# A new step order for a pipelined linear-attention and mixture-of-experts block on one core

## The reference

```python
x = x + conv(ln_c(x))            # causal linear attention, 8 heads of 16
t = tokens(x)
t = t + ffn(ln_t(t))             # 8 experts, the best two of each token
# conv: q, k, v = W x + b;  Q, K = elu(.)+1
#   num_l = Q_l . sum_{j<=l} K_j V_j^T ;  den_l = Q_l . cumsum(K)_l
#   (K is summed over the axis that cumsum(axis=1) names: the heads)
# ffn: probs = softmax(xf @ gate_w + router); best two kept as weights
#   out = sum_e combine_e * (gamma_e * (xf @ expert_w[e] + expert_b[e]) + beta_e)
```

## Time and profile before

| what | before |
| --- | --- |
| median of 3 runs | 755.08 us (754.4 to 756.46) |
| the profiled execution's own time | 755.91 us |
| its span | 754.1 us |
| TensorE matmul busy | 717.1 us, 95% |
| VectorE busy | 685.9 us, 91% |
| ScalarE, GpSimd busy | 409.9 us and 397.8 us |
| mean granted TensorE clock | 0.982 of full speed |

### The profile page before, as it was taken

The page is one execution under the profiler, slowest core; times in us unless marked ns, Lnnn a source line. Parts: engine busy times, 40 slices in busy tenths (PEclk is TensorE's granted clock), DMA queues, the critical chain, the costliest instruction groups (busy, mean ns, idle before and its releaser), DMA issues.

```text
span 754.1 us, 23195 instructions
## 1 busy us (share of the span) xinstructions
PE 717.1 (95%) x8137; PEld 624.0 (83%) x8137; DVE 685.9 (91%) x2550; ACT 409.9 (54%) x1261; POOL 397.8 (53%) x639
## 2 busy tenths in 40 slices
PE   4767999999999999999999999999999999999986
PEld 2666888888888888888888888888888888888875
DVE  4567999999999999999999999999999999999984
ACT  1122666655555666666665555555555555555544
POOL 5145555555555555555555555555555555555520
PEclk9769999999999999999999999999999999999999
DMA  5101111111111111111111111111111111111101
GB/s 129 33 15 30 42 40 35 37 40 37 39 37 42 42 42 42 42 42 42 42 42 42 42 42 42 42 42 42 42 42 42 42 42 42 42 30 29 30 16 29
DMA packets 60214, 30.29 MB, mean 40 GB/s; under 512 B 2160, under 2 KB 60176, under 8 KB 60176
## 3 DMA queue, kind: packets, MB, share of 16 engines
q1 hardware_dynamic: 60176, 29.79, 14.4%
HBM read 20.34 MB, written 9.44 MB: 39 GB/s over the span
## 4 chain that ended last, share of the span: by engine, by line
PE 91%; DVE 4%; POOL 2%; ACT 1%; issue 1%; DMA 1%; SPq 0%; DVEq 0%; ACTq 0%; POOLq 0%
PE bank L877 11%; PE bank L915 10%; PE bank L894 9%; PE bank L916 9%; PE bank L917 9%; PE bank L933 8%; PE bank L901 4%; PE bank L909 4%; PE bank L884 4%; PE bank L853 3%; PE bank L854 3%; PE bank L855 3%; PE bank L860 3%; PE bank L847 2%; PE bank L866 2%; PE bank L935 2%
## 5 line engine op out<-in xcount | busy, mean ns | idle before, releaser
L574 DVE TENSOR_TENSOR probs<-bank,tri 128x512 f32<-128x512 f32 x288 | 184.9, 684 | 10.2 <-PE bank L877 4.7
L397 ACT ACTIVATE y_act<-bank,scale 128x128 f32<-128x128 f32 x576 | 159.4, 383 | 2.5
L915 PE MATMUL bank<-e_high,x_high 128*128 128x512 f32 x288 | 124.0, 431 | 1.1 <-DVE o L803 1.1
L916 PE MATMUL bank<-e_low,x_high 128*128 128x512 f32 x288 | 113.7, 395 | 0.0
L917 PE MATMUL bank<-e_high,x_low 128*128 128x512 f32 x288 | 113.5, 394 | 0.0
L311 POOL TENSOR_TENSOR qn<-feat,rden 128x512 f32<-128x512 f32 x36 | 38.2, 1061 | 116.4 <-DVE rden L672 116.4
L416 ACT ACTIVATE x_high<-x 128x512 fp32r<-128x512 f32 x36 | 22.8, 633 | 137.0 <-DVE x L664 137.0
L592 DVE SCALAR_TENSOR_TENSOR y_dve<-bank,scale,y_dve 128x128 f32<-128x128 f32 x288 | 92.4, 343 | 0.0
L580 DVE SCALAR_TENSOR_TENSOR qkv<-bank,rstd,b_qkv 128x384 f32<-128x384 f32 x144 | 86.8, 605 | 5.1 <-POOL rstd L301 2.6
L387 ACT ACTIVATE k_odd<-bank,parity 128x512 f32<-128x512 f32 x36 | 24.7, 687 | 114.4 <-PE bank L860 114.4
L933 PE MATMUL bank<-ident,y_act 128*128 128x128 f32 x576 | 80.8, 273 | 1.6 <-ACT y_act L397 1.6
(11 more groups left out here) (139 smaller groups left out, 1764.5 us busy)
## 6 DMA issues: line engine op xcount, KB each, us to landing
x<-in_x SPq DMA_DIRECT2D x36, 256.0 KB, 3.3
x_res<-in_x SPq DMA_DIRECT2D x36, 256.0 KB, 3.2
out<-o SPq DMA_DIRECT2D x36, 256.0 KB, 2.4
beta_raw<-in_L_ffn_beta_w SPq DMA_DIRECT2D x1, 512.0 KB
e_raw<-in_L_ffn_expert_w SPq DMA_DIRECT2D x1, 512.0 KB
w_raw<-in_L_conv_Wkv SPq DMA_DIRECT2D x2, 64.0 KB, 2.4
b_qkv<-in_L_conv_bkv SPq DMA_DIRECT2D x1, 128.0 KB, 4.4
w_raw<-in_L_conv_Wq SPq DMA_DIRECT2D x1, 64.0 KB, 2.6
```

The lines of the kernel that those rows point to most:

```text
L397: last = nc.scalar.activation(y_act[:, p, u, e], bank[EXPERTS_AT[u][0]][:, 128 * e:128 * e + 128], ACT.Copy, scale=scale[:, p, u, e:e + 1])
L574: return tt(probs[:, half, i].rearrange("p u e t -> p (u e) t"), bank[SCORES_AT[half][i]][:].rearrange("p (n t) -> p n t", t=T), tri[:].un ...
L915: mm(out, x1_high[:, p, u], e_high[:, w], start=True, stop=False)
L916: mm(out, x1_high[:, p, u], e_low[:, w], start=False, stop=False)
```

## The change

Every engine's step gets another order, and the banks are dealt out anew. TensorE's list in one step after: turn_k; values_1, values_0; proj_2, proj_0; experts_01; proj_1; turn_x1; experts_00, 11; proj_3; turn_q; turn_x of g[1]; experts_31, 21, 20; scores_1 of g[3]; experts_30; turn_coef; experts_10; key_values; from_state of g[3]; bias; scores_0 of g[3]; turn_y of units 2 and 3, then of units 0 and 1. So `scores_0` and `from_state` move from g[4] to g[3], and `turn_x` with its moments and `x_high` from g[0] to g[1]. The products are the same in number and size.

```diff
-AT = dict(x=4, kv=3, att=6, x1_a=6, x1_b=4, k=1, q=7, coef=0, out=1)
-PROJ_AT = (4, 0, 3, 2)
-SCORES_AT = ((3, 7, 2, 0), (0, 5, 6, 7))
-EXPERTS_AT = ((4, 2), (6, 5), (1, 1), (2, 3))
+AT = dict(x=5, kv=5, att=4, x1_a=0, x1_b=5, k=1, q=6, coef=3, out=0)
+PROJ_AT = (7, 3, 1, 4)
+SCORES_AT = ((3, 2, 7, 6), (1, 5, 7, 6))
+EXPERTS_AT = ((1, 2), (7, 7), (3, 4), (2, 0))
...
-            def turn_y(p, u):
-
-                out = bank[AT["out"]][:, T * u:T * u + T]
-                for e in range(4):
-                    mm(out, y_act[:, p, u, e], ident[:], start=False, stop=False, is_transpose=True,
-                       skip_group_check=True)
-                return mm(out, y_dve[:, p, u], ident[:], start=False, stop=True, is_transpose=True,
-                          skip_group_check=True)
+            def turn_y(p, half):
+
+                for e in range(5):
+                    for u in (2 * half, 2 * half + 1):
+                        last = mm(bank[AT["out"]][:, T * u:T * u + T], y_act[:, p, u, e] if e < 4 else y_dve[:, p, u],
+                                  ident[:], start=False, stop=(e == 4), is_transpose=True, skip_group_check=True)
+                return last
```

TensorE's waits of the new order that the text speaks of:

```diff
+                    need(pe, "y_dve_12", n - 1)
+                    need(pe, "y_act_0", n - 1)
+                    scores(p, 1).then_inc(S["scores_1"], 1)
...
+                    need(pe, "probs_12", n + 3)
+                    experts(p, 1, 0).then_inc(S["experts_10"], 1)
...
+                    need(pe, "probs_11", n + 1)
+                    key_values(p).then_inc(S["kv"], 1)
+                    need(pe, "y_dve_22", n - 1)
+                    from_state(p).then_inc(S["from_state"], 1)
```

More of the change, by code:

```diff
@@ L177, in program @@
         names = ("consts setup first_loaded rest_loaded first_pe first_dve rest_pe rest_dve x_eps x1_eps "
[4 rows of a table removed]
-                 "rank_b qkv_0 rank_b_max soft_scaled den_eps hot_b x1 hot_ab rden scale coef qkv_3 x_moments "
[5 rows of a table removed]
-                 "k_sum_3 x_rstd k_sum_4 k_sum_5 k_sum_6 k_sum_7 qk qn state coef_low x_low x1_rstd ").split()
+                 "k_turned values_1 values_0 proj_2 proj_0 experts_01 proj_1 x1_turned experts_00 experts_11 "
+                 "proj_3 q_turned x_turned experts_31 experts_21 experts_20 scores_1 experts_30 coef_turned "
+                 "experts_10 kv from_state bias scores_0 y_turned_b y_turned_a rank_b_max x1 qkv_2 hot_b soft "
+                 "den hot_ab soft_scaled den_eps qkv_0 rden coef scale x1_parts qkv_1 x1_moments qkv_3 "
[3 rows of a table added]
+                 "probs_01 out psum_r rank_b kv_new k_even k_odd x_high x1_high y_one_0 coef_high lg_raw_a "
+                 "lg_raw_b y_one_1 q_t y_act_0 y_one_3 exps_1 y_one_2 y_act_2 exps_0 y_act_3 coef_t y_act_1 "
+                 "v_pad_0 v_pad_1 k_sum_0 pexp x_low k_sum_2 k_sum_3 k_sum_4 k_sum_5 k_sum_6 k_sum_7 qk qn "
+                 "coef_low x1_low x1_rstd state x_rstd k_sum_1 ").split()
         S = {n: sem(n) for n in names}
@@ L777, in step @@
                 if g[3]:
-                    n = g[3].i
-                    need(dve, "scores_1", n + 1)
-                    causal(1, 1).then_inc(S["probs_11"], 1)
-                    causal(1, 0).then_inc(S["probs_10"], 1)
+                    causal(0, 1).then_inc(S["probs_01"], 1)
+                if g[5]:
+                    n, p = g[5].i, g[5].par
+                    need(dve, "y_turned_a", n + 1)
+                    need(dve, "y_turned_b", n + 1)
+                    if not isinstance(n, int) or n >= PAR:
+                        dve.wait_ge(stored[p], 16 * g[5].half)
+                    tt(flat(o, p), bank[AT["out"]][:], flat(x1, p), ALU.add).then_inc(S["out"], 1)
                 if g[4]:
@@ L879, in scores @@
                 return last
-            def from_state(p):
-                for u in range(U):
-                    last = mm(bank[AT["att"]][:, T * u:T * u + T], state[:, U * p + u], q_t[:, p, u],
-                              start=(u == 0), stop=False, skip_group_check=True)
-                return last
             def values(p, half):
@@ L895, in values, with from_state @@
                                       probs[:, half, i, v, e], start=False, stop=(e == 1), skip_group_check=True)
+                return last
+            def from_state(p):
+                for u in range(U):
+                    last = mm(bank[AT["att"]][:, T * u:T * u + T], state[:, U * p + u], q_t[:, p, u],
+                              start=(u == 0), stop=False, skip_group_check=True)
                 return last
@@ L1054, in step @@
                     turn_q().then_inc(S["q_turned"], 1)
+                if g[1]:
+                    n, p = g[1].i, g[1].par
+                    pe.wait_ge(x_loaded[p], 16 * (g[1].half + 1))
+                    need(pe, "lg_raw_b", n - 2)
+                    if k is not None:
+                        need(pe, "x_parts", n)
+                    turn_x(p).then_inc(S["x_turned"], 1)
+                if g[5]:
+                    n, p = g[5].i, g[5].par
+                    need(pe, "x1_parts", n + 2)
+                    need(pe, "lg_raw_a", n + 2)
+                    if k is not None:
+                        need(pe, "out", n)
+                    experts(p, 3, 1).then_inc(S["experts_31"], 1)
+                    need(pe, "qkv_3", n + 4)
+                    if k is not None:
+                        need(pe, "x1", n + 2)
+                        need(pe, "y_one_2", n)
+                        need(pe, "y_dve_22", n)
+                    experts(p, 2, 1).then_inc(S["experts_21"], 1)
+                    need(pe, "qkv_1", n + 4)
+                    if k is not None:
+                        need(pe, "probs_00", n + 2)
+                        need(pe, "coef_t", n)
+                    experts(p, 2, 0).then_inc(S["experts_20"], 1)
@@ new lines, in step @@
+                if g[3]:
+                    n, p = g[3].i, g[3].par
+                    need(pe, "probs_13", n + 1)
+                    need(pe, "y_act_3", n - 1)
+                    need(pe, "y_act_1", n - 1)
+                    if k is not None:
+                        need(pe, "qkv_1", n + 2)
+                        need(pe, "probs_01", n)
+                        need(pe, "probs_12", n + 1)
+                        need(pe, "qkv_0", n + 2)
+                    scores(p, 0).then_inc(S["scores_0"], 1)
```

597 lines of the change are left out of this document (267 added, 330 removed), and 12 rows, old and new, of the table names.

## The result

The changed kernel takes 761.02 us, median of five executions (758.07 to 762.63); the kernel before took 755.08 (754.09 to 757.15). The ratio is 1.0069, with a 95% interval of 1.0048 to 1.0090: the change makes the kernel 0.7% slower. I had forecast 751.0, with 746.5 to 760.0 as the range.

A forecast was written before the change was run, and what follows sets the result against it. TensorE was taken to set the 19.22 us step, with VectorE 0.7 us behind. Span 754.1 + 4.0 (waits) - 1.3 (fill) - 6.8 (drain) = 750.0, so 751.0 us on the median, range 746.5 to 760.

The forecast's parts named there:

- Edges of tiled blocks and kinds of products: TensorE's list: three entries into tiled blocks before and after, so grouping saves 0; bounds 0.2 us a step either way.
- Alternating transposes: turn_y on TensorE: in-place adding transposes cost the same 0.109 us, so alternating units gains 0.
- Waits behind turn_x: Full steps: TensorE waits for VectorE at scores_1 and key_values, 0.13 us a step; +4.0 us, bounds 0 and +9.3.
- The fill: Before the full steps: rest-of-weights starts sooner and step 5 in effect at 69.7 for 70.3; -1.3 us, bounds -3 and +1.
- The drain: Last steps: shorter chains, no mask wait of 1.74 us, last two o 9.8 us apart; -6.8 us, bounds -4 and -8.
- is already there: Step 40 in the drain: rank_b done early, five router operations off the path to scale; last interval 9.8 for 10.9, -1.1.
- rival (d): Port shared by VectorE's rank_b and GpSimd's qk: 1.15 us blocked a step, 760 us if not absorbed; chance 0.22.
- lg0 behind `state`: A possible second port conflict each step, VectorE's lg0 behind GpSimd's state: 31 x 1.15 us more, some 795.
- The sum: Whole kernel: 754.1 + 4.0 - 1.3 - 6.8 = 750.0 us span, 751.8 profiled, 751.0 on the median.

The follow-up runs named there:

- e8: The edits of e2, e5 and e6 together in the changed kernel; 755.40 us, 0.9995 of the kernel before.
- e7: Changed kernel with turn_y going unit by unit again instead of alternating; 762.09 us, 1.0101 of the kernel before.
- e2: Changed kernel with the wait for y_dve_12 moved behind the other waits at scores_1; 756.55 us, 1.0010 of the kernel before.
- e3: Changed kernel with the four extra waits of the unrolled steps at scores_1 also in the loop; 768.93 us, 1.0165 of the kernel before.
- e12: Changed kernel plus 48 products nobody reads, ahead of TensorE's waits in the fill; 754.36 us, 0.9985 of the kernel before.
- e13: Kernel before plus 47 products nobody reads, where TensorE waits in steps 2 to 5; 752.33 us, 0.9938 of the kernel before.
- e1: The changed kernel run again without edits, for a second profile; 761.31 us, 1.0061 of the kernel before.
- e6: Changed kernel with rank_b and psum_r moved up on VectorE to right behind psum; 758.93 us, 1.0054 of the kernel before.
- e10: e8 with the router's exponential pexp ahead of y_act_1 on ScalarE; 756.58 us, 1.0004 of the kernel before.
- e14: e10 plus unread products in the fill, and in the drain the last but one o behind the last group's scale; 749.79 us, 0.9906 of before.
- e4: Changed kernel with two pairs of VectorE weighings swapped so y_dve_12 ends sooner; 758.10 us, 1.0019 of the kernel before.
- e5: e4 with the mask probs_11 also moved up on VectorE, right behind probs_12; 756.16 us, 1.0011 of the kernel before.

## Why the prediction was wrong

- **Edges of tiled blocks and kinds of products, 0.** Right. The changed list's blocks last what the earlier trace rows said, and with the waits repaired (e8) a step is 19.26 us against 19.22.
- **Alternating transposes, 0.** Right (e7): 2.24 us either way. The 2.28 of the earlier trace rows has an entry into tiles in it (0.10); the 2.24 has none, but comes out of tiles, and its first five transposes take 0.60 us where the next five take 0.55.
- **Waits behind turn_x, +4.0 us.** The mechanism was right, the place and the size were not. I had scores_1 late by 0.04 and key_values by 0.09, and took 0.13 with the weight load added; scores_1 is late by 0.18 in the loop (2.81 for 2.63) and by 0.35 in the unrolled steps, and key_values comes just in time behind it. Measured: 26 x 0.16 + 4 x 0.34 = +5.6. Left out of the sum were the semaphore instructions behind the late wait, 0.105 us each, which e2 takes away and e3 multiplies. y_dve_12 itself came 0.25 before scores_1, and 0.15 of it remain with its wait in last place. from_state, to which I gave 0.1 us to spare, is the third in line: once the two ahead of it were repaired it came 0.06 late (e8).
- **The fill, -1.3 us. This step failed most:** it measured +0.8 in the first profile and +3.4 on the average. The earlier start was there (rest-of-weights at 13.70 for 15.94, I had said up to 2 us and taken 0.7), and scores_1 of group 1 came at 60.19 for the 62.5 of my sum. But from there to values_0 I summed 1.1 + 1.4 + 1.7 + 1.1 + 2.7 = 8.0 us, and it is 12.04 (60.19 to 72.23). Of the 4.0, 2.6 go away with the products of e12 (9.47), so they are TensorE's clock: cold blocks of which I took the full-clock durations. Of the remaining 1.4, 0.9 stand between scores_1 and key_values (61.73 to 65.11 in e12, 3.38 for 2.5), where lg0 is held up by the port. The kernel before loses about as much by the clock in its own fill; there I had used measured starts that already held it (e13).
- **The drain, -6.8 us.** Half right: -4.2. The wait of 1.74 us for masks is gone, as forecast. The steps came out longer by little each: step 36 19.53 (19.2), step 37 18.99 (18.8), step 38 17.83 (17.0), step 39 13.19 to its `o` (13.0), the last interval 10.11 (9.8). And 0.7 us lie behind the start of the last `o`, 4.20 us for 3.46. It is 4.12 in e1 and 3.45 in e12, whose drain has the same list, so this one profile does not tell what the order costs there; the three profiles with the list before (e13 is one) all have 3.46. I did not settle it. Step 38's 0.8 are x1, which no projections cover any more (turn_x1 waits 0.5), turn_q (0.2) and scores_1 (0.2). That rank_b "is already there" was wrong: it stood behind psum, which waited for pexp, and behind `o` (742.03, then 742.73). But e6, e10 and e14 show that this cost 0.3 us at most.
- **The port, rival (d).** For rank_b its place and its price were right (1.25 us, in 12 of 36 steps), and that it hides in VectorE's idle time as well: x1 comes up to 0.5 us later, and the steps get no longer. What I had only named in passing, lg0 behind `state`, comes once, in the fill, and there TensorE waits for what stands behind it (e13). The Trainium skill, SBUF — State Buffer, section "Who interferes with whom", has the second of two such instructions wait until the first is done; the trace agrees where rank_b starts 0.065 to 0.083 us behind qk (305.51 and 305.43). Where it starts up to 0.06 us behind (247.49 and 247.48, or 111.21 and 111.15) it was second as well, and took 0.15 to 0.16; there the measurement differs from the rule.
- **The sum.** 751.0 was forecast, 761.0 came: 4.7 from the fill (3.4 for -1.3), 2.6 from the drain, 1.6 from the waits, and 0.8 because I took the profiled execution of before to lie above its median, which later medians of 755.8 to 756.5 don't bear out; 9.7 of 10.0. All errors have one sign. As work moved from the drain to the fill, their sum is the safer figure: -8.1 forecast, -0.8 measured. The 760 of rival (d) lay near by luck: its cost in the full steps was nothing.

What stays open: why the stretch of rest-of-weights lasts 10.0 to 12.3 us from one execution to the next, what else makes the spread of e12's executions, and what in the changed list's fill costs the 1.9 us beyond the moved work.

## What to carry to other kernels

When a wait may come late, give it the last place of all waits at that instruction: those behind it are worked off only afterwards, and here that alone was 2.9 us in 30 steps. When one late result is repaired, look for the next in line before counting the gain (e4 gave 3.1 us in 30 steps, e5 4.4, and a third wait stood behind those two). And cost fill and drain by their own rows, clock included; in a short kernel cheap products in TensorE's waits can be worth as much (0.6 to 0.9% here) as the order of the steps (0.7%).

## What the runs showed of the hardware

- A semaphore instruction behind a late wait costs TensorE 0.105 us, and its row is 51 ns long; a register operation between them (e3, 32 ns long) adds 0.09. With the late wait last, the distance from the end of VectorE's instruction to the first product was 0.15 us (e2).
- A VectorE operation on 32 numbers from two SBUF tiles took 1.25 to 1.27 us where it started 0.065 to 0.083 us behind GpSimd's qk, and 0.15 to 0.16 where it started 0.061 or less behind (the 36 rank_b of the first profile).
- Products that nobody reads raised the granted clock over steps 3 and 4 from 0.64 and 0.82 to 0.90 and 1.00 and shortened these two steps from 37.8 to 34.2 us, although they stand in TensorE's own list ahead of what it waits for.
